# Attention maxima in a ring of three PSUM banks, one reduction per head, carried to the query's row straight from their columns

## The reference, cut to what matters

```
scale = D ** (-0.5)
q, k, v = jnp.split(qkv, 3, axis=-1)
attn = jnp.einsum('bihd,bjhd->bijh', q, k) * scale
attn = jax.nn.softmax(attn, axis=2)
out = jnp.einsum('bijh,bjhd->bihd', attn, v).reshape(bs, n, HEADS * D)
...
valid = (ki >= qi + 1) & (ki <= qi + w)
scores = jnp.where(valid[None, None], scores, neg)
attn = jax.nn.softmax(scores, axis=-1)
...
gate_logits = x @ gate_weight.T
```

## Time and profile before

| | us |
|---|---|
| median of 3 runs | 867.62 (866.97 to 867.73) |
| the profiled execution's time | 864.95 |
| its span, first to last instruction | 863.2 |
| the `attend` stage within it | about 77 to 420 |
| PE, DVE, ACT, POOL busy over the span | 688.5, 612.1, 418.2, 424.5 |

### The profile page before, as it was taken

The page is one execution under the profiler, slowest core; times in us unless marked ns, Lnnn a source line. Parts: engine busy times, 40 slices in busy tenths (PEclk is TensorE's granted clock), DMA queues, the critical chain, the costliest instruction groups (busy, mean ns, idle before and its releaser), DMA issues. The chain is left out here.

```text
span 863.2 us, 21250 instructions
## 1 busy us (share of the span) xinstructions
PE 688.5 (80%) x7173; PEld 521.9 (60%) x7173; DVE 612.1 (71%) x1648; ACT 418.2 (48%) x829; POOL 424.5 (49%) x560
## 2 busy tenths in 40 slices
PE   0658899999999999997746998784988787359994
PEld 0234566666666666665545887762666666349993
DVE  3765578788877777876598888767567776647764
ACT  0355466665655544553264666520766666134442
POOL 0236102222227888879405777702555787724551
PEclk9979999999999999999566999985999999669995
DMA  6740000000000000000001222413400000122216
GB/s 175 225 164 1 2 3 2 3 3 3 2 3 4 3 15 15 21 16 21 25 1 34 53 53 54 47 7 106 119 2 2 14 17 17 53 68 72 65 46 195
DMA packets 42316, 37.39 MB, mean 43 GB/s; under 512 B 8947, under 2 KB 34536, under 8 KB 42212
## 3 DMA queue, kind: packets, MB, share of 16 engines
q1 hardware_dynamic: 35300, 24.55, 10.0%
q0 software_dynamic: 4800, 9.40, 4.8%
q10 hardware_dynamic: 2112, 2.10, 0.8%
HBM read 26.76 MB, written 9.46 MB: 42 GB/s over the span
## 5 line engine op out<-in xcount | busy, mean ns | idle before, releaser
L782 DVE TENSOR_REDUCE attend_negmax<-ps 128x4 f32<-128x1024 f32 (+1 forms) x128 | 139.6, 1090 | 82.9 <-PE ps L586 82.2
L729 ACT ACTIVATE attend_prob<-ps 128x1024 f32<-128x1024 f32 (+1 forms) x128 | 110.7, 865 | 137.2 <-PE ps L596 137.2
L586 PE MATMUL ps<-attend_key,attend_query 32*128 32x256 f32 (+2 forms) x1024 | 124.8, 360 | 12.8 <-DVE attend_negmax L782 11.6
L596 PE MATMUL ps<-attend_query,attend_key 32*128 32x256 f32 (+2 forms) x1024 | 124.6, 359 | 1.1 <-ACT attend_prob L729 1.0
L586 PEld LDWEIGHTS ps<-attend_key,attend_query 32*128 32x128 f32 x1024 | 79.6, 184 | 53.5 <-issue 45.7
L1777 POOL DMA_INDIRECT sums_xs<-table,sums_source x79 | 76.6, 969 | 56.8 <-DVE sums_source L1710 33.0
L596 PEld LDWEIGHTS ps<-attend_query,attend_key 32*128 32x128 f32 x1024 | 88.3, 184 | 2.3 <-issue 2.2
L1495 PE MATMUL ps<-sums_xT,sums_own 128*128 128x128 f32 x632 | 84.0, 279 | 0.0
L1495 PEld LDWEIGHTS ps<-sums_xT,sums_own 128*128 128x128 f32 x632 | 78.3, 195 | 0.0
L522 POOL TENSOR_SCALAR attend_rstd<-attend_spread 128x2 f32<-128x2 f32 x32 | 7.5, 234 | 130.7 <-DVE attend_spread L837 130.7
L1838 ACT ACTIVATE sums_hidden<-ps 128x512 f32<-128x512 f32 x79 | 47.2, 597 | 34.2 <-PE ps L1495 34.1
(11 more groups left out here) (346 smaller groups left out, 1616.7 us busy)
## 6 DMA issues: line engine op xcount, KB each, us to landing
attend_query<-attend_negmaxT SPq DMA_DIRECT2D x512, 0.5 KB
w<-in_L_ffn_w SPq DMA_DIRECT2D x1, 4096.0 KB, 27.9
expert_xs<-slots SPq DMA_DIRECT2D x39, 64.5 KB, 1.9
x<-in_x ACTq DMA_DIRECT2D x4, 512.0 KB, 8.3
table<-rows SPq DMA_DIRECT2D x16, 128.0 KB
experts<-in_L_ffn_W SPq DMA_DIRECT2D x1, 2048.0 KB, 8.7
experts<-in_L_ffn_W SPq DMA_DIRECT2D x4, 512.0 KB, 9.6
rows<-outputs SPq DMA_DIRECT2D x8, 256.0 KB, 4.9
```

Source lines behind the costliest of these rows:

```text
L586: return nc.tensor.matmul(ps[:, SCORE + i, at:at + width], query[rows, n % 3, odd, a * 128:(a + 1) * 128], key[rows, n % 3, odd, from_:fro ...
L596: return nc.tensor.matmul(ps[:, KEY_SCORE + i, at:at + width], key[rows, n % 3, odd, b * 128:(b + 1) * 128], query[rows, n % 3, odd, from_ ...
L729: nc.scalar.activation(of_pair(t // 4, t % 4)[:, :, 0:wide], ps[:, KEY_SCORE:KEY_SCORE + 2, 0:wide], ACT.Exp).then_inc(prob_ready, 1)
L782: last = nc.vector.tensor_reduce(out=negmax[:, s % 2, 0:4].rearrange("p (a r) -> p r a", a=2), in_=ps[:, SCORE:SCORE + 2, 0:2 * width].rea ...
```

## The change

The score banks become a ring of three: head i of slot s uses bank (2s + i) mod 3, so PE waits only for the maximum of the first head of the slot before. The third bank was that of the gate logits, which move into the bank of `turn_rows`; they go from j = 2 to j = 0 on PE and from j = 3 to j = 1 on DVE, and `turn_rows` gains a wait for them. DVE takes one maximum per head, two reductions a slot in place of one, and no longer transposes them. SP moves each maximum from its column of 128 partitions straight into the query's row: in full-attention slots two DMAs of 128 pieces of 8 bytes (even and odd queries beside each other, for which `by_query` loads every second query as its stationary operand), in windowed slots four DMAs of 128 pieces of 4 bytes. Each DMA now waits for its own head's maximum, and a maximum waits until the one four slots earlier has been placed.

```diff
-    SCORE, KEY_SCORE, PROJECT, HEADS, TURN, MISC = 0, 2, 4, 5, 6, 7
+    SCORE, KEY_SCORE, PROJECT, HEADS, TURN = 0, 3, 5, 6, 7
-        negmax = sb("negmax", [128, 2, 32])
-        negmaxT = sb("negmaxT", [128, 4, 32])
+        negmax = sb("negmax", [128, 4, 2, 2])
+        def score_bank(s, i):
+            return SCORE + (2 * s + i) % 3
...
-                    sp.wait_ge(max_turned, s + 1)
                     for i in range(2):
                         row = free_row(groups[i], odd)
+                        sp.wait_ge(max_ready, 2 * s + i + 1)
+                        if not windowed(n):
+                            sp.dma_start(query[row:row + 1, n % 3, odd, :], negmax[:, s % 4, i, :])\
+                                .then_inc(max_placed[s % 4], 16)
+                            continue
                         for a in range(2):
                             sp.dma_start(query[row:row + 1, n % 3, odd, a * 128:(a + 1) * 128],
-                                         negmaxT[2 * a + i::32, s % 4, :]).then_inc(max_placed[s % 4], 16)
+                                         negmax[:, s % 4, i, a:a + 1]).then_inc(max_placed[s % 4], 16)
...
                         if s >= 1 and not windowed(n):
-                            pe.wait_ge(max_ready, s)
+                            pe.wait_ge(max_ready, 2 * s - 1)
...
-                        return nc.tensor.matmul(ps[:, SCORE + i, at:at + width],
-                                                query[rows, n % 3, odd, a * 128:(a + 1) * 128],
+                        own = slice(a * 128, (a + 1) * 128) if windowed(n) else slice(a, N, 2)
+                        return nc.tensor.matmul(ps[:, score_bank(s, i), at:at + width],
+                                                query[rows, n % 3, odd, own],
...
                 def mask_scores(s, columns):
                     if s >= 1:
-                        pe.wait_ge(max_ready, s)
+                        pe.wait_ge(max_ready, 2 * s - 1)
...
                 def turn_rows(n):
+                    if n - 1 >= IMAGES:
+                        pe.wait_ge(logits_taken, n - IMAGES)
...
                 def maximum(s):
-                    dve.wait_ge(scored, 2 * s + 2)
+                    if s >= 4:
+                        dve.wait_ge(max_placed[s % 4], placed(s // 4))
                     width = 192 if windowed(s // 4) else 256
-                    last = nc.vector.tensor_reduce(out=negmax[:, s % 2, 0:4].rearrange("p (a r) -> p r a", a=2),
-                                                   in_=ps[:, SCORE:SCORE + 2, 0:2 * width].rearrange(
-                                                       "p r (a n) -> p r a n", a=2),
-                                                   axis=AX.X, op=ALU.max, negate=True)
-                    last.then_inc(max_ready, 1)
+                    for i in range(2):
+                        dve.wait_ge(scored[i], s + 1)
+                        nc.vector.tensor_reduce(out=negmax[:, s % 4, i, :],
+                                                in_=ps[:, score_bank(s, i), 0:2 * width].rearrange(
+                                                    "p (a n) -> p a n", a=2),
+                                                axis=AX.X, op=ALU.max, negate=True).then_inc(max_ready, 1)
-                def turn_max(s):
...
-                    nc.vector.transpose(negmaxT[:, s % 4, :], negmax[:, s % 2, :]).then_inc(max_turned, 1)
```

More of the change, by code:

```diff
@@ L415, in attend @@
         vaug_ready = sem("vaug_ready")
-        scored = sem("scored")
+        scored = [sem(f"scored{i}") for i in range(2)]
         max_ready = sem("max_ready")
-        max_turned = sem("max_turned")
         max_placed = [sem(f"max_placed{r}") for r in range(4)]
@@ L458, in tiles, with placed @@
             return (2 * (m % 2), 2 * (m % 2) + 1), m // 2
+        def placed(k):
+            return 32 * min(k, IMAGES) + 64 * max(k - IMAGES, 0)
         def free_row(group, odd):
@@ L500, in _ @@
                 signals.clear(pool)
-                pool.wait_ge(zeros_set, 4)
+                pool.wait_ge(zeros_set, 3)
                 for t in range(0, TILES, 8):
@@ L605, in score_pairs @@
                                 if piece == pieces[1]:
-                                    mm.then_inc(scored, 1)
+                                    mm.then_inc(scored[i], 1)
                     if t >= 0:
-                        pe.wait_ge(max_placed[t % 4], 64 * (t // 4 + 1))
+                        pe.wait_ge(max_placed[t % 4], placed(t // 4 + 1))
                         if t >= 1:
@@ L619, in mask_scores @@
                     if s >= 1:
-                        pe.wait_ge(max_ready, s)
+                        pe.wait_ge(max_ready, 2 * s - 1)
                     for i in range(2):
                         for c in range(0, 128, columns):
-                            nc.tensor.matmul(ps[c:c + columns, SCORE + i, 0:384], window_mask[:, 0:128][:, c:c + columns],
+                            nc.tensor.matmul(ps[c:c + columns, score_bank(s, i), 0:384], window_mask[:, 0:128][:, c:c + columns],
                                              window_mask[:, 128:512], start=True, stop=False)
@@ L668, in gate_logits @@
                     for a in range(2):
-                        mm = nc.tensor.matmul(ps[:, MISC, a * E2:(a + 1) * E2],
+                        mm = nc.tensor.matmul(ps[:, TURN, a * E2:(a + 1) * E2],
                                               rowsT[:, k % 2, a * 128:(a + 1) * 128], gate[:, :], start=True,
@@ L686, in _ @@
                             project_out(n - 4)
+                        if runs(n - 6) and windowed(n - 6):
+                            gate_logits(n - 6)
                     if j == 1 and runs(n - 2):
@@ L691, in _ @@
                             project(n + 1)
-                        if runs(n - 6) and windowed(n - 6):
-                            gate_logits(n - 6)
                         if runs(n - 5):
@@ L763, in take_values @@
                     if n == 0:
-                        dve.wait_ge(zeros_set, 3)
+                        dve.wait_ge(zeros_set, 2)
                     if n >= 3:
@@ L871, in _ @@
                             invert_sums(n - 3)
+                        if runs(n - 6) and windowed(n - 6):
+                            take_logits(n - 6)
                     if j == 2:
@@ L879, in _ @@
                             turn_normed(n - 3)
[L880 to L883, removed]
                     choose(s)
```

10 lines of the change are left out of this document (2 added, 8 removed).

## The result

The changed kernel takes 884.62 us (median of 4 runs, 882.88 to 886.18) against 867.3 of the kernel before beside it: ratio 1.0207, interval 1.0176 to 1.0238. It is slower by some 17 us, where 14 us less was forecast.

A forecast was written before the change was run, and what follows sets the result against it. PE's waits for DVE's maximum were the prize, limited by ACT's chain; 11.2 us from windowed images plus 2.9 from full attention, off the median 867.62, gave 853.5 us. Own range 849 to 858, with rivals 843.5 to 868.

The forecast's parts named there:

- SP's issues: Windowed part: 17 issues at 0.477 us take 8.1 us an image, below the 9.09 us that the image needs.
- the small pieces bind: Rival: SP's 17 windowed issues at 0.62 us take 10.5 us an image, so slower, 876.7 us; chance 0.15.
- Its second mechanism: Within the 0.15 rival: writes into a single partition, if run one after another, also make it slower, at more.
- The maximum per head: Windowed part: reducing one head's 384 columns takes 0.55 us; the round over the mask becomes 1.93 us.
- One windowed image: Windowed part: 9.09 us with gate product against 9.79, 8.69 without against 9.39; 11.2 us in 16 images.
- Full attention: Full-attention images: the long round falls from 2.52 to 2.34 us, 0.18 us an image, 2.9 us in 16.
- The sum: Whole kernel: 11.2 + 2.9 = 14.1 us off, 853.5 us on the median.
- DVE's work: Attention slots on DVE: load stays even, 8.05 us an image, 89% of a 9.09 us one; free.
- the logits: Gate logits' copy in slot 1 on DVE: 1.9 us of PE work covers the wait of `turn_rows`; taken as 0.
- Every second query as stationary operand: Full-attention score loads: stepping costs at most 66 ns more each, 17 us in all; taken as 0.
- The rivals that priced the strided loads and DVE: Strided loads cost 44 ns apiece, 11 us, 867.6, chance 0.05; DVE's small steps lose half the windowed gain, 859.1, chance 0.13.
- all of PE's waiting comes off: Rival: PE's whole wait for DVE's maximum in the stage goes, 22.4 us, to 845.2 us; chance 0.10.

The follow-up runs named there:

- e9: Changed kernel with windowed DMAs of 4, 16, 32 and 128 pieces of 4 bytes in slots 0 to 3 of an image; 878.79 us, 1.0153.
- e13: Changed kernel with windowed DMAs carrying zeros in another form per slot (4-, 128-, 64-, 16-byte pieces, partitions adjacent or 32 apart); 869.11 us, 1.0032.
- e1: Changed kernel with only partitions 0 to 63 of each windowed DMA moved, 64 pieces in place of 128; 882.39 us, 1.0176.
- e2: Changed kernel with one windowed DMA of 256 pieces a head in place of two of 128; 852.56 us, 0.9840.
- e5: Changed kernel with only partitions 0 to 7 of each windowed DMA moved, 8 pieces of 4 bytes; 881.03 us, 1.0171.
- e3: Changed kernel with the last of a slot's four windowed DMAs issued from ACT's queue in place of SP's; 850.40 us, 0.9816.
- e4: The hybrid: changed kernel, but windowed slots carry their maxima through DVE's transpose as the kernel before did; 852.68 us, 0.9835.
- e8: Changed kernel with the transposed carry in every slot, so only the ring, the maximum per head and the moved logits remain; 851.05 us, 0.9842.
- e6: Changed kernel with eight columns of maxima and eight semaphores in place of four; 881.87 us, 1.0199.

## Why the prediction was wrong

**The step that failed** is "SP's issues". It took 433 ns from the one load of `w_wq_r`, because that load has the same piece size, added 44, and got 8.1 us an image, below the 9.09 of the image that it forecast. Measured: 601 + 44 ns, 10.97 us, and 11.6 with the write of rows. The load wasn't cheap for want of a queue; it began 0.04 us behind the end of an issue, and the two behind it took 0.61 and 0.58 us:

```profile
1.27 0.42 SPq L2253 DMA_DIRECT2D const_prep<-in_const_prep  x1
1.73 0.43 SPq L2255 DMA_DIRECT2D w_wq_r<-in_L_conv_wq_r  x1
2.20 0.61 SPq L2255 DMA_DIRECT2D w_wv_r<-in_L_conv_wv_r  x1
2.85 0.58 SPq L2255 DMA_DIRECT2D w_w_up<-in_L_conv_w_up  x1
```

It was another form: an input that goes into 128 partitions, where the new DMAs take their pieces out of 128 partitions into one. The size of a piece, for which it was picked, isn't what sets the price (e9, e13), and it is a single issue; the other one at hand said 576. The new form takes 469 ns by itself, and 601 in a queue without gaps. Why the load took no more than 433 stays open. The 17 issues filled 9.1 of 9.79 us already in the kernel before, so this was the term with the least room, and one issue of another form wasn't fit to price it. The first of its unknowns, the price of a piece, hardly mattered (e1, e2, e5).

**The rival that happened** is "the small pieces bind", with 0.62 us an issue and 876.7 us, at 0.15. Its place and its sign were right and 0.62 was close to 0.645. What it lacked: the long issue (with 0.645 for 0.62 that makes 11.6 us an image, not 10.5) and, the other way, that the first images run ahead of SP; together the 8 us up to 884.6. Both signs that it had been given, SP back to back and DVE waiting for `max_placed`, are in the trace. The reason in its name was wrong: neither their size nor, but for a little, their number sets the period (e1, e2, e5, e13). Its second mechanism, writes into one partition that run one after another, is ruled out by e2 and e3.

The Trainium skill spoke for this rival in DMA: Bandwidth & Descriptors, section Rules for kernel authors. The sign agrees; the reason, a descriptor per element, does not: 256 elements a DMA in half as many DMAs gave 852.56 us, 128 gave 884.62. The Trainium skill, Perfetto Trace Analysis, section What "DMA-bound" means, names an issuing engine's track that is solid with DMA slices as a bound of its own; here that is the row of 17 issues in 11.85 us. The Trainium skill, DMA: Bandwidth & Descriptors, section Issuing engines are not separate DMA queues, says that other queues save only the time of issue, usually small beside the DMA itself. Here it was small beside the DMA, 0.60 us against a landing of 2.0, and yet the loss, and e3 got it back.

**The rest held.** *The maximum per head*: 0.55 us for 384 columns; 553 ns measured:

```profile
L795 DVE TENSOR_REDUCE attend_negmax<-ps 128x2 f32<-128x384 f32 x128 | 65.4, 553 | 56.8 <-DMA attend_query<-attend_negmax 43.4 <-PE ps L596 13.4
...
L795 DVE TENSOR_REDUCE attend_negmax<-ps 128x2 f32<-128x512 f32 x128 | 82.5, 686 | 47.1 <-PE ps L596 47.0
```

*One windowed image*: 9.09 and 8.69 forecast, 9.10 with the gate product in e2, where SP is out of the way, and 8.73 to 8.74 without it in the change itself, before SP falls behind. Slot 3 in e2:

```profile
319.97 0.71 ACT L741 ACTIVATE attend_prob<-ps 128x640 f32<-128x640 f32 x1
...
329.07 0.72 ACT L741 ACTIVATE attend_prob<-ps 128x640 f32<-128x640 f32 x1
...
338.18 0.71 ACT L741 ACTIVATE attend_prob<-ps 128x640 f32<-128x640 f32 x1
```

The steps fit as well as the sum: in e2 it is 2.98 us from the projection to that exponential (forecast 3.01), 1.97 for slot 1 (1.96), and the key products of slot 0 start 0.15 us after the exponential's end (0.1). *Full attention*: 2.34 us in the long round. *The sum* without SP's term: 853.5 forecast, 852.68 (e4), 851.05 (e8). *DVE's work* and *the logits* at nothing: in e3 and e2 DVE is busy for 41.07 of 50 us and PE loses 0.07. *Every second query as stationary operand* at nothing: in full attention (110 to 235 us) such a load takes 191 ns in the change, 184 in e8, which loads queries that lie side by side:

```profile
L596 PEld LDWEIGHTS ps<-attend_key,attend_query 32*128 32x128 f32 x400 | 35.5, 191 | 14.8 <-issue 11.0 <-DVE attend_negmax L795 1.7
```
```profile
L595 PEld LDWEIGHTS ps<-attend_key,attend_query 32*128 32x128 f32 x400 | 34.1, 184 | 14.8 <-issue 11.1 <-DVE attend_tall L797 1.5
```

These 7 ns, of 66 at most, cost nothing: images of full attention take 9.91 us in both. The rivals that priced the strided loads and DVE did not occur (the first was also added up wrongly: 853.5 + 11 is 864.5, not 867.6). Of *all of PE's waiting comes off* half came true: PE's idle time went, to 0.07 of 50 us in e3, but the time stayed at 850.4 where 845.2 had been put, so idle time that goes is not time gained one for one.

## What to carry to other kernels

Count the issues of a queue against the time of the loop that they serve, before anything else about a DMA: at 17 an image and half a microsecond each, a fifth more apiece made the queue the bound. Take the price from many issues of the same form, source partitions included, that stand back to back, never from a single one. Where a queue is the limit, fewer DMAs with more pieces (e2), a second issuing queue (e3), or sources on partitions 32 apart (e4, e8) help; deeper buffers don't (e6).

## What the hardware showed that I had not expected

An issue of many pieces can make the next one on SP dearer, one of another form too: the write of finished rows, whose form the change doesn't touch, went from 440 to 591 ns in the median (L492 above; the row of the kernel before is the first below). In e5, behind 8 pieces, it stays at 441 (the second). It isn't so for all: the loads `const_prep` and `w_wq_r` above took 0.42 and 0.43 us, each right behind a load to 128 partitions.

```profile
L482 SPq DMA_DIRECT2D table<-rows x16: 360/440/450, 305.0 to 421.8; - x16
```
```profile
L492 SPq DMA_DIRECT2D table<-rows x16: 359/441/468, 310.1 to 438.2; - x16
```

The long issues of 0.9 to 1.7 us coincide with the core's loads of instructions. In the trace's DMA records of the changed kernel's windowed part, each of 17 issues over 0.8 us overlaps one of the 17 transfers of 16 KB (0.9 to 1.4 us each) on the instruction queue; a stretch of 1.8 us around one of them, by queue (packets, MB, share):

```profile
q1 hardware_dynamic: 414, 0.00, 12.4%
q8 instruction: 1, 0.02, 4.6%
```

The hybrid has 18 such transfers and no long issue, e5 (8 pieces) 17 and four long ones, e1 (64 pieces) 17 and 17; in e9 the 12 long ones fell on DMAs of 16 pieces and more, none on those of 4. So the number of pieces matters there, or something that goes with it. The cause is inferred from the coincidence alone; no run moved the loads.
